# Bias rows of layers 1 to 3 as rounded high and low parts in one product, with the calls of all engines in a new order

## What is computed

```python
mod = (silu(c) @ wmod).reshape(16, 6, 1, 128)
sa, ca, ga, sb, cb, gb = (mod[:, k] for k in range(6))
h = layernorm(x) * (1 + ca) + sa
x = sqrt(128) * h + positions
for l in range(4):
    h = layernorm(x) * ln1_s[l] + ln1_b[l]
    q, k, v = h @ Wq[l] + bq[l], h @ Wk[l] + bk[l], h @ Wv[l] + bv[l]
    x = x + linear_attention(elu(q) + 1, elu(k) + 1, v) @ Wo[l] + bo[l]
    h = layernorm(x) * ln2_s[l] + ln2_b[l]
    x = x + relu(h @ W1[l] + b1[l]) @ W2[l] + b2[l]
```

## Time and profile before

| what | value |
|---|---|
| median of 3 runs | 592.32 us (590.99 to 592.59) |
| the profiled execution | 592.54 us, of which its span is 590.7 us |
| PE busy | 567.1 us, 96% of the span, 4578 records |
| DVE, ACT, POOL busy | 73%, 66%, 44% of the span |
| chain that ended last, by engine | PE 86%, ACT 4%, POOL 3%, DVE 3%, issue 3%, transfers 1% |
| PE's granted clock | 1.00 in every stretch |

### The profile page before, as it was taken

One profiled execution on the slowest core, in us unless ns is written; L12 is line 12 of the kernel. 1 busy time (PEld: TensorE's weight loads), 2 busy tenths in 40 slices (PEclk: granted clock), 3 DMA queues, 4 the chain that ended last, 5 costly groups with the idle time before them and its releaser, 6 DMA issues.

```text
span 590.7 us, 13153 instructions
## 1 busy us (share of the span) xinstructions
PE 567.1 (96%) x4578; PEld 536.1 (91%) x4578; DVE 432.6 (73%) x1476; ACT 392.6 (66%) x1392; POOL 259.9 (44%) x431
## 2 busy tenths in 40 slices
PE   6999999999999999998999999999999999999997
PEld 4578899998999999998999999998999999999886
DVE  5857667777886776777986777767897666667785
ACT  3777588886666676687594666687675656656651
POOL 4344387554413356553513346745422344435420
PEclk9999999999999999999999999999999999999999
DMA  6800420220000000000000000000000000000000
GB/s 198 235 6 0 159 70 20 102 79 2 19 2 19 2 2 1 2 2 2 2 19 19 1 1 1 2 1 2 2 19 19 1 3 1 1 2 2 1 19 18
DMA packets 11041, 15.58 MB, mean 26 GB/s; under 512 B 968, under 2 KB 8220, under 8 KB 10592
## 3 DMA queue, kind: packets, MB, share of 16 engines
q1 hardware_dynamic: 8896, 12.52, 6.8%
q0 software_dynamic: 448, 1.25, 0.7%
q10 hardware_dynamic: 1632, 0.98, 0.6%
HBM read 12.61 MB, written 2.14 MB: 25 GB/s over the span
## 4 chain that ended last, share of the span: by engine, by line
PE 86%; ACT 4%; POOL 3%; DVE 3%; issue 3%; DMA 1%; SPq 0%; POOLq 0%; DVEq 0%
PE psB L1585 20%; PE psD L1585 20%; PE psC L1585 20%; PE psA L1585 19%; PE psC L1657 1%; PE psA L1657 1%; PE psB L1657 1%; PE psD L1657 1%; DMA wm<-in_wmod 1%; PE psB L1708 1%; PE psC L1708 1%; PE psD L1708 1%; PE psA L1708 1%; ACT kpB L494 0%; ACT xhiC L435 0%
## 5 line engine op out<-in xcount | busy, mean ns | idle before, releaser
L825 POOL TENSOR_TENSOR rstdC<-msC,neghalf 128x2 f32<-128x2 f32 x20 | 14.0, 699 | 89.3 <-ACT eqkC L458 50.3
L825 POOL TENSOR_TENSOR rstdA<-msA,neghalf 128x2 f32<-128x2 f32 x20 | 14.0, 700 | 44.1 <-ACT eqkA L458 40.2
L1585 PE MATMUL psB<-w,H 128*128 128x128 f32 x256 | 31.4, 276 | 0.0
L1585 PE MATMUL psD<-w,H 128*128 128x128 f32 x256 | 31.4, 276 | 0.0
L1585 PE MATMUL psA<-w,H 128*128 128x128 f32 x256 | 31.2, 275 | 0.0
L1585 PE MATMUL psC<-w,H 128*128 128x128 f32 x256 | 31.1, 275 | 0.0
L1585 PEld LDWEIGHTS psC<-w,H 128*128 128x128 f32 x256 | 30.0, 192 | 0.0
L1585 PEld LDWEIGHTS psA<-w,H 128*128 128x128 f32 x256 | 30.0, 192 | 0.0
L1585 PEld LDWEIGHTS psD<-w,H 128*128 128x128 f32 x256 | 29.8, 191 | 0.0
L1585 PEld LDWEIGHTS psB<-w,H 128*128 128x128 f32 x256 | 29.8, 191 | 0.0
L458 ACT ACTIVATE eqkA<-xA 128x129 f32<-128x129 f32 x64 | 19.3, 305 | 15.1 <-DVE xA L1166 7.9
(11 more groups left out here) (576 smaller groups left out, 2366.4 us busy)
## 6 DMA issues: line engine op xcount, KB each, us to landing
M<-modulation_rows SPq DMA_DIRECT2D x2, 1280.0 KB, 7.9
M<-modulation_rows SPq DMA_DIRECT2D x1, 2560.0 KB, 9.2
out<-X SPq DMA_DIRECT2D x16, 128.0 KB, 1.9
M<-in_attn_W SPq DMA_DIRECT2D x3, 256.0 KB, 3.3
X<-in_attn_x_in ACTq DMA_DIRECT2D x2, 256.0 KB, 3.5
M<-in_attn_W ACTq DMA_DIRECT2D x1, 256.0 KB, 3.7
wo<-in_attn_Wo POOLq DMA_DIRECT2D x1, 256.0 KB, 3.7
wm<-in_wmod SPq DMA_DIRECT2D x1, 256.0 KB, 2.8
```

Of the source, the lines that this page charges most:

```text
L825: pool.tensor_tensor(b.rstd[:, :], b.ms[:, :], neghalf[:, :], ALU.pow).then_inc(b.s_rstd.sem, 1)
L1585: return pe.matmul(o, lhsT, rhs, start=start, stop=stop)
```

## The change

The bias rows are loaded into two partitions instead of one, each with the same values. For layers 1, 2 and 3 ACT rounds both rows (896 columns: 384 and 512) into a buffer of two partitions in float32r (`bias_high`), and DVE then makes of it (`bias_low`) the rounded row in one partition and the remainder in the other. `unit` has two partitions, so that one float32r product of two rows adds high and low part. The buffers are two of the experts' weight tiles, `wgu_hi` and `wgu_lo`, which are not used yet. Layer 0 keeps its float32 product with one row. So six float32 products become six float32r products, and ACT and DVE get three instructions each. A fold of layer l now waits for `bias_low(l)`. The rest of the diff is order: calls move in the lists of PE, ACT, DVE and POOL, in the beginning and in all steps.

```diff
-        bias = flat(M[:, :, :])[0:1, 0:LAYERS * (QKV + FF)].rearrange("p (l n) -> p l n", n=QKV + FF)
+        bias = flat(M[:, :, :])[0:2, 0:LAYERS * (QKV + FF)].rearrange("p (l n) -> p l n", n=QKV + FF)
...
-        unit = sb("unit", [1, P])
+        unit = sb("unit", [2, P], F32R)
+        minus_hi = base[0:2, 1:2]
...
+        bias_parts = [w[0:2, :, :, :].rearrange("p k c n -> p (k c n)")[:, 0:QKV + FF] for w in (wgu_hi, wgu_lo)]
...
-            sync.dma_start(bias[:, :, QKV:], b1.rearrange("(a l) n -> a l n", a=1)).then_inc(s_bias, 16)
+            sync.dma_start(bias[:, :, QKV:], b1.rearrange("(a l) n -> a l n", a=1).to_broadcast([2, LAYERS, FF])).then_inc(s_bias, 16)
...
+            def bias_high(l):
+
+                act.wait_ge(s_bplus, 2)
+                if l == 3:
+                    act.wait_ge(s_foldps, 4)
+                act.activation(bias_parts[l % 2], bias[:, l, :], ACT.Copy).then_inc(s_condT, 1)
...
+            def bias_low(l):
+
+                dve.wait_ge(s_condT, 4 + l)
+                dve.scalar_tensor_tensor(bias_parts[l % 2], bias_parts[l % 2], minus_hi, bias[:, l, :],
+                                         ALU.mult, ALU.add).then_inc(s_bplus, 1)
...
-                if k == 0:
-                    pe.wait_ge(s_bplus, min(l, 1) + 1)
+                pe.wait_ge(s_bplus, 1 if l == 0 else 2 + l)
...
-                mm(b.ps[:, 1, 0:width], unit[:, :], bias[:, l, first:first + width], start=False).then_inc(s_foldps, 1)
+                mm(b.ps[:, 1, 0:width], *((unit[0:1, :].bitcast(F32), bias[0:1, 0, first:first + width]) if l == 0 else
+                                          (unit[:, :], bias_parts[l % 2][:, first:first + width])), start=False).then_inc(s_foldps, 1)
...
             for i in range(STEPS):
-                if i == 0:
-                    fold_weights(3)
                 transposes(D_, i, 0)
+                transposes(A, i, 1)
                 transposes(C, i, 0)
-                transposes(A, i, 1)
+                transposes(B, i, 1)
                 project_keys(D_, i, 0)
                 project_queries(D_, i, 0)
-                transposes(B, i, 1)
...
+                contract(A, i, 1)
                 transposes(B, i, 3)
-                contract(A, i, 1)
```

More of the change, by code:

```diff
@@ L528, in _ @@
             key_exps(B, 0, 0)
-            high(1)
+            bias_high(1)
             query_exps(B, 0, 0)
+            centre(C, 0)
             less_wo_means(0)
@@ L533, in _ @@
             squares(D_, 0, 1)
-            centre(C, 0)
+            squares(C, 0, 1)
             att_transposed(B, 0, 0)
-            squares(C, 0, 1)
+            high(1)
             high(2)
@@ L566, in _ @@
                 transposed(C, i, 1)
-                squares(D_, i, 2)
                 if i == 0:
@@ L570, in _ @@
                 key_exps(A, i, 1)
+                query_exps(A, i, 1)
                 transposed(B, i, 2)
-                query_exps(A, i, 1)
+                squares(D_, i, 2)
                 relu(C, i, 0, 0)
@@ L585, in _ @@
                     high(6)
-                    less_wo_means(2)
+                squares(C, i, 3)
                 squares(A, i, 4)
@@ L682, in _ @@
                 query_exps(C, i, 3)
+                squares(B, i, 8)
                 transposed(D_, i, 6)
@@ L1330, in _ @@
             masked(B, 0, 0)
-            low(1)
+            bias_low(1)
             divided(B, 0, 0)
@@ L1356, in _ @@
                 divided(D_, i, 0)
+                scale(A, i, 3)
                 if i == 0:
                     low(4)
-                scale(A, i, 3)
                 move(B, i, 2)
+                if i == 0:
+                    bias_low(3)
                 low_part(A, i, 2)
-                move(D_, i, 1)
                 low_part(C, i, 1)
                 scale(B, i, 3)
-                if i == 0:
-                    low(5)
+                move(D_, i, 1)
                 positive_keys(A, i, 1)
@@ L1375, in _ @@
                 divided(A, i, 1)
-                move(C, i, 2)
                 positive_queries(B, i, 1)
@@ L1387, in _ @@
                 low_part(C, i, 2)
-                move(B, i, 3)
                 low_part(A, i, 3)
@@ L1448, in _ @@
                 masked(D_, i, 2)
+                if i + 1 < STEPS:
+                    in_scale(C, i + 1)
+                scale(A, i, 7)
                 move(C, i, 5)
-                scale(A, i, 7)
                 divided(D_, i, 2)
@@ L1473, in _ @@
                 move(A, i, 7)
+                scale(C, i, 7)
                 divided(B, i, 3)
-                scale(C, i, 7)
                 move(D_, i, 6)
@@ L1510, in _ @@
                 route(AB, i, 1)
+                move(D_, i, 8)
                 gate_up(A, i, 2)
-                move(D_, i, 8)
                 gate_up(B, i, 2)
@@ L1857, in _ @@
                 expand(B, i, 0, 0)
+                sums(D_, i, 0)
                 attend(C, i, 0)
@@ L1878, in _ @@
                 expand(C, i, 0, 1)
-                transposes(D_, i, 1)
                 sums(A, i, 1)
@@ L1991, in _ @@
                 project_queries(C, i, 3)
+                sums(C, i, 3)
                 transposes(D_, i, 6)
-                sums(C, i, 3)
                 contract(A, i, 3)
@@ L2020, in _ @@
                 gate(B, i, 2)
+                up(B, i, 2)
+                contract(D_, i, 3)
+                gate(B, i, 0)
                 gate(A, i, 0)
-                contract(D_, i, 3)
-                up(B, i, 2)
-                gate(B, i, 0)
                 up(A, i, 0)
@@ L2044, in _ @@
                 logits2(D_, i)
-                if i + 1 < STEPS:
-                    transposes(A, i + 1, 0)
+                gate(D_, i, 2)
                 logits2(C, i)
@@ L2083, in _ @@
                     out_project2(B, i + 1, 0)
+                spread(C, i, 1)
+                spread(D_, i, 1)
                 down(D_, i)
```

344 lines of the change are left out of this document (177 added, 167 removed).

## The result

The changed kernel takes 588.77 us (median of 5 runs, 587.52 to 589.16) against 592.32 (5 runs, 590.99 to 593.46): 3.55 us less, ratio 0.9941, 95% interval 0.9924 to 0.9958. Forecast were 586.3 us with a range of 583.8 to 590.4 and a chance of 0.82 for faster. The time lies in the range and is faster by more than 0.3%; but it is 2.5 us above the number, and lies at what the first rival gave (588.7). The profiled execution took 587.52, with a span of 585.7, which is the shortest of the five.

A forecast was written before the change was run, and what follows sets the result against it. PE was taken to bound the kernel, busy 96% of the span. Savings of 2.94 + 0.9 + 0.7 + 1.65 = 6.19 us from 592.54 gave 586.3 us, range 583.8 to 590.4.

The forecast's parts named there:

- the first rival: Whole order of calls: the new order gives nothing, only the products shorten; 588.7 us, chance 0.20.
- a. Folds 4 to 7: Layers 2 and 3, dense PE stretch: one-pass bias products save 1.47 us a layer, 2.94 in all.
- b. The beginning: Folds 2 and 3, layer 1: products save 1.47, fold 2 stays 0.35 to 0.8 late; gain 0.9 us (0.4 to 1.5).
- the sign of being wrong, over 1 us: Fold 2 in the beginning: the forecast for it is wrong if PE waits over 1 us for `guA`.
- c. The issues: Expert-weight issues on POOL moved before B's power in layer 1: waits of PE and ACT go, 0.7 us gained.
- The cover: PE, layer 1: `contract(A, 0, 1)`, 1.95 us, now ahead of B's transposes, covers their coming 0.9 later.
- d. The turns: Three turns of the step: exchanged calls fill PE's gaps, 0.55 us a turn, 1.65 in all (0 to 3.4).
- the second place: At each turn, between D's and C's transposes, 0.79 us idle: A's transposes of the next norm use 0.22 of it.
- The third: Roundings on ACT and remainders on DVE delay copies PE waits for, and the order gives nothing; 591.6 us, chance 0.10.
- The fourth: At each turn A's transposes wait for POOL's chain of powers, at worst 3 us a turn; slower, 597 us, chance 0.06.
- The second: Bias products: the new product isn't cheaper, costing two passes as now; 590.7 us, chance 0.05.
- the rule on the shared port: DVE with two SBUF inputs and POOL reading SBUF exclude each other: `bias_low` some 0.45 us longer, sum 586.8.

The follow-up runs named there:

- the second comparison: The changed kernel run once more without an edit, beside the kernel before: 589.17 us, ratio 0.9947.
- issues only: Kernel before with only the seven expert-weight issues moved on POOL, ahead of the power of B in layer 1: 592.39 us, ratio 0.9993.
- selectors: Changed kernel with the cast of the selectors on POOL moved back behind the fold matrices: 589.07 us, ratio 0.9947.
- B's transposes: Changed kernel with the selectors' cast back and, in all steps, B's transposes before the first feed-forward layer back behind D's keys and queries: 589.80 us, ratio 0.9957.
- step 0: Changed kernel, selectors' cast back; in step 0 only, B's transposes behind D's keys and queries, fold 3's low part behind D's on DVE: 588.69 us, ratio 0.9937.
- router: Changed kernel with A's transposes again between the router products of D and C, and D's gate behind B's queries, at each turn: 588.83 us, ratio 0.9932.

## Why the prediction was right, and where it was wrong

**a. Folds 4 to 7: mechanism right, mis-sized.** Forecast 2.94; the products gave 2.24, and the order took 0.24 of it. The step that failed is "by columns, 384 take 0.18 and 512 take 0.24". The changed kernel's rows:

```profile
28.83 0.50 PE L1610 MATMUL psB<-wgu_lo,unit 2*128 2x512 f32 x1
29.26 0.44 PE L1682 MATMUL psD<-K,xnD 128*128 128x128 f32 x2
```

so 0.43 for 512 columns, and 26.42 - 26.05 = 0.37 for 384. Both are 0.19 above the price by columns: a fixed cost, the same in both widths, which a row of equal products in succession can't show. Whether the float32 product ahead of it or its two rows make it is not shown. The saving per layer is (0.84 - 0.37) + (1.05 - 0.43) = 1.09, for two layers 2.18, close to the 2.24 measured.

**b. The beginning: the wait right, its terms mis-sized.** Forecast 0.9 (0.4 to 1.5). Of the unedited kernel 1.99 and 0.67 were measured, and in two more profiles in which the beginning is the same 1.10 and 0.65: 1.1 in the mean. The terms were otherwise. The saving of the products is 1.09, not 1.47. I had fold 2 late by ACT's copy `guA`, and so it is, although the profile's brackets name POOL and DVE (the rows of fold 2 above). But PE idles 0.84 and 1.03 in the two profiles, not 0.35 to 0.8, and the sign of being wrong, over 1 us, is met by 0.03 in the second. A's transposed attention, the input of the copy, was there at 23.54 and 24.59, and the copy began 1.13 and 1.41 later; with the order alone, which rounds no bias rows, it began 0.82 later, so most of this is the rest of what was put ahead of it, C's centring above all. ACT's rounding took 0.93 to 0.95 (forecast 0.94), DVE's remainder 1.13 (forecast 1), and it was done in time.

What made up for it is that PE had A's attention transposed 1.98 and 0.93 earlier than before (25.52), where up to 1.4 was forecast. So fold 2 starts at 25.24 and 26.57 (before: 26.22), and the whole 1.32 between the two profiles is there at this point. With one term too large, one wait too small and a start that varies by over 1 us, it is in part luck that 0.9 came out near the mean.

**c. The issues: right.** Forecast 0.7, measured 0.78 to 0.82. The wait of PE for the power of A and that of ACT for the last transfer (the row of ACT above) are gone; A's transposes follow C's after 0.22:

```profile
87.14 0.38 PE L1682 MATMUL psC<-K,xnC 128*128 128x128 f32 x2
87.36 0.38 PE L1682 MATMUL psA<-K,xA 128*128 128x128 f32 x2
```

The cover was right in kind, since without the contraction ahead the issues cost 0.56 at B's transposes; but I had priced the exchange itself at nothing, and alone it costs 1.3 us a step. "Costed at nothing" was right only because other calls moved with it.

**d. The turns: wrong.** Forecast 1.65; nothing was gained. Step 1 is 0.2 shorter, but so it is with the products alone, in the old order. The changed kernel at the second turn, against the earlier trace rows:

```profile
290.00 0.51 PE L1610 MATMUL psD<-wr,kpD 128*128 128x8 f32 x4
290.37 0.37 PE L1610 MATMUL psD<-xhiD,wgu_hi 128*128 128x256 f32 x1
290.57 0.28 PE L1610 MATMUL psD<-xhiD,wgu_lo 128*128 128x256 f32 x1
290.91 0.39 PE L1610 MATMUL psD<-xloD,wgu_hi 128*128 128x256 f32 x1
291.13 0.54 PE L1610 MATMUL psC<-wr,kpC 128*128 128x8 f32 x4
...
293.79 0.38 PE L1682 MATMUL psA<-K,xnA 128*128 128x128 f32 x2
293.93 0.37 PE L1610 MATMUL psB<-xhiB,wqkv_hi 128*128 128x256 f32 x1
294.13 0.28 PE L1610 MATMUL psB<-xhiB,wqkv_lo 128*128 128x256 f32 x1
```

The statement that failed is "`gate(D_, i, 2)`, which has its inputs": its third product starts 0.34 after the second instead of 0.12, and it is the one that needs `xloD`. A's transposes cost at their new place what they cost elsewhere: 0.14, and the product behind them 0.20, together 0.34, which is the 0.22 of a pair and the 0.12 of a product. So the gap was filled with a call that waits there itself: D's expert products (`psD<-wd,H`) come 20.60 us after those of B, where they came 20.61 after. At the second place, now and, in the single line, before (beside the earlier trace rows):

```profile
310.39 0.38 PE L1682 MATMUL psD<-K,xnD 128*128 128x128 f32 x2
310.95 0.44 PE L1682 MATMUL psA<-K,xA 128*128 128x128 f32 x2 [0.18 <-POOL xA L837]
311.40 0.44 PE L1682 MATMUL psC<-K,xnC 128*128 128x128 f32 x2
311.68 0.38 PE L1682 MATMUL psB<-K,xB 128*128 128x128 f32 x2
311.81 0.36 PE L1610 MATMUL psD<-wqkv_hi,xhiD 128*128 128x256 f32 x1
```

```profile
316.80 0.36 PE L1585 MATMUL psD<-wqkv_hi,xhiD 128*128 128x256 f32 x1
```

C's transposes come 1.01 after D's, as before, and D's keys 1.42 after, as before. A and B lie in the gap, and B's move there is worth the 0.24 a turn that its removal cost. This part of the forecast held, but the step didn't keep it: counted from B's expert product, B's contraction (`psB<-w,H`) comes 0.18 earlier than before in layer 0 of the next step, 0.07 in layer 1, 0.10 in layer 2 and 0.01 in layer 3. Which of the exchanges in the layers cost it wasn't tried one by one.

That PE is busy 0.49 us longer per step is no longer work. As an estimate from the starts: over what each kind of product usually takes to the next start (0.11 to 0.12 for most), a step has 7.3 us of late starts in both kernels. The profile shows 2.96 of them as idle before and 2.47 now; the rest lies under the durations of the products ahead, which reach past the next start. Changes between float32 and float32r aren't the cause: there are 86 in a step before and 88 now, and a change is made up for, as 0.14 + 0.20 shows.

**Rivals.** The first gave the right number for a wrong reason: the order is not worth nothing, it gives 0.8 at the issues and lets the products take effect in the beginning, while the products give less than it had. The third (gain given back to waits on ACT and DVE) is what happens with the products in the old order: 1.4 of 3.3 us of saved PE work is left. The fourth (POOL's chain at the turn) shows its wait, 0.18 for `xA`, but far from the 3 us at which it decided; it stands in the old gap. The second fell: all six products are one record.

**The sum.** With the measured sizes: 2.0 (a, less what the order takes) + 1.1 + 0.8 + 0.2 = 4.1 us, a little above the 3.55 of the first comparison and the 3.97 of the second; the forecast was 6.19. The stretches are taken against one profile of the kernel before, of a run of 592.54, which is 0.5 above the median of its runs at that clock (592.04). The two parts of the change don't add up: 1.4 alone and 0.5 alone (which may be nothing), 3.6 to 4.0 together. Of the runs with a mean clock of 0.999 and above alone, it is 1.3 and 0.6, and 2.2 to 3.0 together.

## What to carry to other kernels

Price an instruction by the whole distance to the next start, in the form and the place in which it will stand, and not by its columns from a row of other ones. A gap on a busy engine is worth filling only if what is put in has its inputs; check that the length of the step falls, since busy share can rise with nothing gained: a start that comes a little late hides under the product ahead. The name in brackets is a guess at what ended a wait: compare the ends of everything that the call waits for, and take the one whose distance to the start stays the same from run to run. In a hand-written order a single exchange has no price of its own: ask what it covered before, and move the calls that depended on that cover with it.

## What the runs showed of the hardware

**A copy of one column took 0.88 us beside the remainder.** In the first profile of the changed kernel, POOL and DVE:

```profile
23.21 0.63 POOL L817 TENSOR_SCALAR M<-K,parT 128x127 f32<-128x127 f32 x1
23.81 0.88 POOL L818 COPY M<-parT 128x1 f32<-128x1 f32 x1
...
23.50 1.13 DVE L1022 SCALAR_TENSOR_TENSOR wgu_lo<-wgu_lo,K,M 2x896 fp32r<-2x896 f32 x1
```

The other copies of this line have a median of 0.187 us; this one ended at 24.69, DVE's remainder at 24.63. (Fold 2 waits for both, but `guA` came later.) I had weighed the rule on the shared port (the Trainium skill, SBUF — State Buffer, "SBUF: two separate sides") as one that lengthens the remainder by 0.45. It agrees, but with the loser on the other side: DVE came first, and POOL was held. That the remainder has only two partitions didn't help. It took 1.13 to 1.14 everywhere but in two places: with the old products and the new order its first took 1.33 and with the products alone its third 1.23, both begun while POOL was at an addition of 256 columns, and POOL's next instruction took 1.45 and 1.46, where 0.63 and 0.7 are usual. So the remainder was lengthened by 0.20 and 0.10 there, never by 0.45. In the rows above it began while POOL was busy as well, and wasn't longer.

**The clock fell although PE was busy.** In two of four profiles with the old order in the beginning (products alone, and issues only) PE's granted clock fell to half from about 17 to 23.5 us. Of the kernel with the products alone:

```profile
16.00:17.00 1.00, 1.00 (x5) 0.28 (x4) 0.48 (x2) 0.11 (x2) 0.81 (x1) 0.95 1.02 307
17.00:18.00 1.00, 1.00 (x3) 0.16 (x3) 0.43 (x1) 0.95 (x2) 0.03 (x1) 0.50 1.02 299
...
23.00:24.00 1.00, 1.00 (x7) 1.00 (x7) 0.79 (x3) 0.19 (x1) 0.83 (x3) 0.64 1.06 291
```

PE had been busy in every us from 10 to 17. In the kernel with the issues only, whose beginning is that of the kernel before, the same drop made the beginning 0.97 us longer. It was in neither of the other two profiles with that beginning, and in none of the ten with the new one.

The mean granted clock of each run tells more (one run of the kernel before at 0.75, 712.41 us, is left out). Of 76 runs of the kernel before 27 have 0.993, as the profile of the issues only, with a median of 593.5; the other 49, at 0.999 or 1.00, have 592.04. So the drop comes in about one run in three of one and the same kernel, and goes with 1.5 us. The Trainium skill, TensorE: Matmul & The Clock Gate, "Part 1: The HAM clock gate", says that the gate's watch runs freely and isn't started by the kernel, so that the same program can meet it differently; these runs agree with that. The changed kernel and its four variants near 589 (selectors, B's transposes, step 0, router) have 35 runs, none under 0.996; nine are at 0.996 or 0.997, and no profile shows where their drop lies. The new order alone doesn't keep the longer drop away: the other four kernels that have it have 7 of 45 runs at 0.991 to 0.994.

At 0.999 and above the changed kernel has a median of 589.06 (8 runs), 3.0 us under the kernel before (49 runs, three chips). On the chip of the second comparison alone it is 589.08 (3 runs) against 591.29 (5 runs), 2.2. So, as an estimate, 0.6 of the 3.55 and 1.8 of the 3.97 us is the drop that the kernel before meets more often (of the first comparison the clock of the runs before isn't listed, the profiled one aside). What in the changed kernel avoids it stays open.
